# A two-layer AdaLN kernel on one core: the attention loop's work is put in another order

## The reference, cut to what matters

```
h = layernorm(x) * (1 + ca) + sa              # ca, sa per batch
q, k, v = h @ wq + bq, h @ wk + bk, h @ wv + bv    # 16 heads of 8
att = softmax(q k^T / sqrt(8)) v              # per head, 512 x 512 scores
x = x + ga * (att @ wo.T + bo)
h = layernorm(x) * (1 + cb) + sb
x = x + gb * experts0(h)                      # softmax router, top tokens per expert
...                                           # layer 1 follows: linear attention, 8 experts
```

## Time and profile before

| | us |
|---|---|
| median of 3 runs | 1118.73 |
| lowest and highest run | 1104.53, 1119.12 |
| span of the profiled execution | 1110.3 |
| busy: PE, PE weight loads | 929.3, 596.8 |
| busy: DVE, ACT, POOL | 759.5, 589.6, 460.1 |

### The profile page before, as it was taken

The page is one execution under the profiler, slowest core; times in us unless marked ns, Lnnn a source line. Parts: engine busy times, 40 slices in busy tenths (PEclk is TensorE's granted clock), DMA queues, the critical chain, the costliest instruction groups (busy, mean ns, idle before and its releaser), DMA issues. The chain is left out here.

```text
span 1110.3 us, 23738 instructions
## 1 busy us (share of the span) xinstructions
PE 929.3 (84%) x7248; PEld 596.8 (54%) x7248; DVE 759.5 (68%) x1948; ACT 589.6 (53%) x1257; POOL 460.1 (41%) x632
## 2 busy tenths in 40 slices
PE   5389898989798998997299899899898789987982
PEld 3023232323232333332298787788788779886761
DVE  2578797878688788889478856655656566663552
ACT  1048677777577676776034435525533475754551
POOL 5121222323231304130424446755752545765772
PEclk9999899999899899999589999999998899998996
DMA  4523232323150515170161001001100112223332
GB/s 134 134 102 88 103 97 98 102 92 108 39 153 14 166 35 168 36 240 12 47 237 58 16 16 34 28 24 30 31 18 18 47 38 61 70 62 106 107 93 76
DMA packets 56332, 87.09 MB, mean 78 GB/s; under 512 B 10388, under 2 KB 41186, under 8 KB 55568
## 3 DMA queue, kind: packets, MB, share of 16 engines
q1 hardware_dynamic: 45392, 53.75, 17.2%
q0 software_dynamic: 10816, 31.84, 8.0%
HBM read 45.83 MB, written 40.24 MB: 78 GB/s over the span
## 5 line engine op out<-in xcount | busy, mean ns | idle before, releaser
L680 DVE TENSOR_REDUCE nmax<-ps_s 128x1 f32<-128x512 f32 x512 | 321.8, 683 | 68.8 <-PE ps_s L861 67.1
L574 ACT ACTIVATE p_ring<-ps_t 128x512 f32<-128x512 f32 x512 | 286.8, 598 | 133.0 <-PE ps_t L872 130.1
L861 PE MATMUL ps_s<-k_stack,q_stack 56*128 56x512 bf16 x512 | 184.6, 409 | 35.2 <-DMA q_stack<-q_parts_dram 16.0
L872 PE MATMUL ps_t<-q_stack,k_stack 59*128 59x512 bf16 x512 | 188.0, 396 | 5.7 <-ACT p_ring L574 2.6
L885 PE MATMUL ps_av<-p_ring,v_ext 128*32 128x256 f32 x2048 | 168.1, 401 | 3.4 <-ACT att L584 2.3
L861 PEld LDWEIGHTS ps_s<-k_stack,q_stack 56*128 56x128 bf16 x512 | 39.9, 94 | 167.8 <-DVE nmax L680 92.0
L1408 POOL DMA_INDIRECT back_dram<-weights,target x78 | 88.3, 1132 | 73.6 <-DVE weights L2018 49.8
L1674 ACT ACTIVATE weights<-a,wtile 128x128 f32<-128x128 f32 x312 | 89.5, 374 | 36.5 <-PE a L2281 35.7
L2292 PE MATMUL a<-wtile,weights 128*128 128x128 f32 x624 | 86.1, 282 | 17.1 <-DVE weights L2018 9.8
L1581 ACT ACTIVATE hid<-a 128x512 f32<-128x512 f32 x64 | 38.2, 598 | 110.0 <-PE a L2103 109.7
L1422 POOL DMA_INDIRECT rows_dram<-hrow,slot x64 | 65.8, 1028 | 74.0 <-DVE y L1772 43.9
(11 more groups left out here) (277 smaller groups left out, 1500.6 us busy)
## 6 DMA issues: line engine op xcount, KB each, us to landing
rows_dram<-wmod POOLq DMA_DIRECT2D x8, 2340.0 KB, 8.5
k_stack<-k_parts_dram SPq DMA_DIRECT2D x32, 192.0 KB
q_stack<-q_parts_dram SPq DMA_DIRECT2D x32, 192.0 KB
xt<-rows_dram SPq DMA_DIRECT2D x78, 65.0 KB, 1.9
wall<-in_wall SPq DMA_DIRECT2D x1, 4112.0 KB, 13.4
q_parts_dram<-q_parts SPq DMA_DIRECT2D x32, 128.0 KB, 2.4
weights<-back_dram SPq DMA_DIRECT2D x8, 512.0 KB, 4.2
k_parts_dram<-k_parts SPq DMA_DIRECT2D x24, 128.0 KB, 2.3
```

Of the source, the lines that this page charges most:

```text
L574: nc.scalar.activation(probs[:, u % RING, :], ps_t[u % TBANKS][:], ACT.Exp, scale=HD ** -0.5).then_inc(exp_done, 1)
L680: nc.vector.tensor_reduce(nmax[:, js, n:n + 1], ps_s[u % SBANKS][:], AX.X, ALU.max, negate=True).then_inc(max_done, 1)
L861: nc.tensor.matmul(ps_s[u % SBANKS][:], q_stack[par][row:row + STACK, c, quarter(t)], k_stack[par][row:row + STACK, c, :], start=True, sto ...
L872: nc.tensor.matmul(ps_t[u % TBANKS][:], k_stack[par][rows_, c, quarter(t)], q_stack[par][rows_, c, :], start=True, stop=True).then_inc(t_f ...
```

## The change

The work of an iteration stands at other places, now named constants (`P_` for PE, `A_` for ACT, `D_` for DVE, with the value of u). `score_t`, the exponentials and `weigh` of unit v are issued on PE at u = v + `LEAD`, with LEAD = 2, so the last two of a batch fall into the next iteration; ACT still counts by its own v, and DVE by u. The statistics and the norm are those of the batch after the next (`statistics_1(nxt + 1)` at u = 31, `norm_1(nxt + 1)` on POOL between two `maxima`), those of batch 0 and 1 both in iteration -1. The projections stand at u = 4, 5 and 10. The copy of v into `v_ext` has moved from DVE to ACT (`save_values`), without the bias: PE computes bv @ wo.T once, DVE adds it to the output bias. Which heads `score` takes at a given u has changed with LEAD, so that `score` and `score_t` of one u still use opposite halves of PE's rows.

```diff
+LEAD = 2
+P_NT = 2
+P_K = 4
+P_Q = 5
+P_V = 10
+P_M1 = 6
+P_H3 = 8
+P_TT = 14
+P_O = 20
+P_M2 = 21
+P_H0 = 23
+P_N2 = 28
+P_LG = 31
+P_M3 = 40
+P_H1 = 44
+P_PT = 47
+P_M0 = 60
+P_H2 = 63
+A_H = 0
+A_K = 2
+A_Q = 5
+A_V = 11
+A_M1 = 4
+A_S3 = 3
+A_TT = 16
+A_S0 = 19
+A_M2 = 20
+A_N2 = 27
+A_S1 = 35
+A_LG = 37
+A_M3 = 40
+A_PT = 49
+A_S2 = 51
+A_M0 = 59
+D_K = 4
+D_Q = 7
+D_N3 = 9
+D_O = 20
+D_N0 = 26
+D_LG = 34
+D_S1 = 31
+D_RT = 45
+D_N1 = 51
+D_N2 = 63
+WEIGH = {1: 0, 3: 1}
+OPPOSITE = (0, 1, 2, 3)
...
-    return (v + 2) % HG
+    return OPPOSITE[v % HG]
...
-        bv = sb("bv", [P, P])
+        bv = sb("bv", [P, B])
...
-            iteration(Batch(B - 2), B % 2)
-            iteration(Batch(B - 1, after=False), (B - 1) % 2)
-            iteration(Batch(B, here=False, after=False), B % 2)
+            iteration(Batch(B - 2, ahead=False), B % 2)
+            iteration(Batch(B - 1, after=False, ahead=False), (B - 1) % 2)
+            iteration(Batch(B, here=False, after=False, ahead=False), B % 2)
...
-            sp.dma_start(bv[:], io["bv"].partition_broadcast(P)).then_inc(wqkv_in, 16)
+            sp.dma_start(bv[:], io["bv"]).then_inc(wqkv_in, 16)
...
 
             def iteration(it, par):
                 b, nxt, prev = it.own, it.own + 1, it.own - 1
-                if it.after:
-                    pool.wait_ge(mv1_done, nxt + 1)
-                    pool.wait_ge(hT_filled, nxt)
-                    norm(nc, half, x_all[:, nxt], mv1, rstd1, r1_step, nxt, xh1, xh1_ready)
+                def norm_1(m):
+                    pool.wait_ge(mv1_done, m + 1)
+                    pool.wait_ge(hT_filled, m)
+                    norm(nc, half, x_all[:, m], mv1, rstd1, r1_step, m, xh1, xh1_ready)
+
+                if it.after and not it.here:
+                    norm_1(0)
                 if it.after and not it.here:
 
                     pool.wait_ge(shift_mm, 1)
@@ -549,6 +598,8 @@
                     norm(nc, half, x_all[:, prev], mv2, rstd2, r2_step, prev, xh2, xh2_ready)
                 if it.here:
                     maxima(b, 3)
+                if it.ahead:
+                    norm_1(nxt + 1)
                 if it.after:
                     maxima(nxt, 0)
 
...
+                def save_values():
+                    act.wait_ge(v_filled, nxt + 1)
+                    if it.before:
+                        act.wait_ge(av_done, H * b)
+                    act.wait_ge(consts, 7)
+                    nc.scalar.copy(v_ext[1 - par][:, :, :, 0:HD],
+                                   bank_a[:].rearrange("p (t h e) -> p t h e", t=NT, h=H)).then_inc(v_ready, 1)
...
-                    work |= {3: lambda: save_av(prev, 3), 17: save_attT, 30: shift_h2, 37: exp_logits, 46: save_probT}
+                    work |= {A_S3: lambda: save_av(prev, 3), A_TT: save_attT, A_N2: shift_h2, A_LG: exp_logits, A_PT: save_probT}
-                    work |= {7: lambda: save_maxima(b, 1, bank_b), 22: lambda: save_maxima(b, 2, bank_b),
-                             38: lambda: save_maxima(b, 3, bank_b), 20: lambda: save_av(b, 0),
-                             35: lambda: save_av(b, 1), 51: lambda: save_av(b, 2)}
+                    work |= {A_M1: lambda: save_maxima(b, 1, bank_b), A_M2: lambda: save_maxima(b, 2, bank_b),
+                             A_M3: lambda: save_maxima(b, 3, bank_b), A_S0: lambda: save_av(b, 0),
+                             A_S1: lambda: save_av(b, 1), A_S2: lambda: save_av(b, 2)}
-                    work |= {8: shift_h, 10: lambda: first_part("k"), 13: lambda: first_part("q"),
-                             57: lambda: save_maxima(nxt, 0, bank_a)}
+                    work |= {A_H: shift_h, A_K: lambda: first_part("k"), A_Q: lambda: first_part("q"), A_V: save_values,
+                             A_M0: lambda: save_maxima(nxt, 0, bank_a)}
...
+                dve.wait_ge(shift_mm, 1)
+                nc.vector.tensor_tensor(vectors[:, 0, :], vectors[:, 0, :], bank_b[0:B, 2 * D:3 * D], ALU.add
+                                        ).then_inc(gate_step, 1)
+                dve.wait_ge(gate_step, 6)
-                dve.wait_ge(shift_mm, 1)
...
-                if it.after:
-                    if not it.here:
-                        dve.wait_ge(x0_in, 16)
-                    elif not it.before:
-                        dve.wait_ge(x_in, 16)
-                    dve.wait_ge(xh1_ready, nxt)
-                    statistics(x_all[:, nxt], st1, mv1, st1_done, mv1_done, nxt)
+                def statistics_1(m):
+                    if isinstance(m, int) and m < 2:
+                        dve.wait_ge(x_in if m else x0_in, 16)
+                    dve.wait_ge(xh1_ready, m)
+                    statistics(x_all[:, m], st1, mv1, st1_done, mv1_done, m)
+
+                if it.after and not it.here:
+                    statistics_1(0)
+                if it.ahead:
+                    work |= {D_S1: lambda: statistics_1(nxt + 1)}
-                    work |= {8: lambda: normalise(prev, 3, bank_b), 20: residual, 33: logits, 40: router}
+                    work |= {D_N3: lambda: normalise(prev, 3, bank_b), D_O: residual, D_LG: logits, D_RT: router}
-                    work |= {25: lambda: normalise(b, 0, bank_a), 43: lambda: normalise(b, 1, bank_a),
-                             59: lambda: normalise(b, 2, bank_b)}
+                    work |= {D_N0: lambda: normalise(b, 0, bank_a), D_N1: lambda: normalise(b, 1, bank_a),
+                             D_N2: lambda: normalise(b, 2, bank_b)}
-                    work |= {10: lambda: rest("k"), 14: lambda: rest("q"), 17: values}
+                    work |= {D_K: lambda: rest("k"), D_Q: lambda: rest("q")}
...
-                if t == 0 and i == 0:
+                if t == 0 and i != 1:
-                some = slice(T // 2 * i, T // 2 * (i + 1))
+                some = slice(0, T) if i is None else slice(T // 2 * i, T // 2 * (i + 1))
-                                            probs[:, (HG * k + g) % RING, some], start=(t == 0 and i == 0),
+                                            probs[:, (HG * k + g) % RING, some], start=(t == 0 and i != 1),
-                if i:
+                if i != 0:
...
-                    free((it.before, avT_read[3], prev + 1), (it.here, m_rows_ready[1], b + 1), (True, mod_ready, 3))
+                    free((it.before, avT_read[2], prev + 1), (it.here, grow_ready, 9), (True, mod_ready, 3))
+                    pe.wait_ge(rest_in, 48)
+                    last = nc.tensor.matmul(bank_b[0:B, 2 * D:3 * D], bv[:], wo[:], start=True, stop=True)
-                    free((it.after, k_rest_ready, nxt + 1))
...
-                    work |= {8: lambda: heads_T(prev, 3, bank_b, (it.here, m_rows_ready[1], b + 1),
+                    work |= {P_H3: lambda: heads_T(prev, 3, bank_b, (it.here, m_rows_ready[1], b + 1),
-                             17: tokens_T, 20: project_o, 30: norm2_T, 33: logits, 45: probs_T}
+                             P_TT: tokens_T, P_O: project_o, P_N2: norm2_T, P_LG: logits, P_PT: probs_T}
-                    work |= {6: lambda: maxima_T(b, 1, bank_b, (it.before, avT_read[2], b), (True, grow_ready, 9)),
-                             21: lambda: maxima_T(b, 2, bank_b, (it.before, attT_ready, prev + 1),
+                    work |= {P_M1: lambda: maxima_T(b, 1, bank_b, (it.after, k_rest_ready, nxt + 1), (True, avT_read[2], b)),
+                             P_M2: lambda: maxima_T(b, 2, bank_b, (it.before, attT_ready, prev + 1),
-                             26: lambda: heads_T(b, 0, bank_a, (it.before, x_ready, prev + 1),
+                             P_H0: lambda: heads_T(b, 0, bank_a, (it.before, x_ready, prev + 1),
-                             36: lambda: maxima_T(b, 3, bank_b, (it.before, h2T_ready, prev + 1),
+                             P_M3: lambda: maxima_T(b, 3, bank_b, (it.before, h2T_ready, prev + 1),
-                             41: lambda: heads_T(b, 1, bank_a, (it.before, lg_ready, prev + 1),
+                             P_H1: lambda: heads_T(b, 1, bank_a, (it.before, lg_ready, prev + 1),
-                             57: lambda: heads_T(b, 2, bank_b, (it.before, probT_ready, prev + 1),
+                             P_H2: lambda: heads_T(b, 2, bank_b, (it.before, probT_ready, prev + 1),
-                    work |= {4: norm_T, 9: project_k, 10: project_q, 15: project_v,
-                             53: lambda: maxima_T(nxt, 0, bank_a, (it.here, avT_read[1], b + 1),
+                    work |= {P_NT: norm_T, P_K: project_k, P_Q: project_q, P_V: project_v,
+                             P_M0: lambda: maxima_T(nxt, 0, bank_a, (it.here, avT_read[1], b + 1),
...
-                    if it.here:
-                        score_t(b, u, par)
-                    if u % HG in (1, 3):
-                        if u < HG and it.before:
-                            weigh(prev, H - 1, 1 - par, u % HG // 2)
-                        elif u >= HG and it.here:
```

(26 more changed lines are left out.)

## The result

The kernel after takes 1060.17 us (median of 4 runs, 1058.66 to 1061.46) against 1111.63 (median of 4, 1102.4 to 1119.12): a ratio of 0.9565, 95% interval 0.9521 to 0.9609. The profiled execution has a span of 1057.5 us against 1110.3, 52.8 less where 29.6 were forecast: 23.2 of the 29 us are gain that the sum missed, and 5.7 are its base, since the prediction put the median 8.4 us above the span and after it stands 2.7 above.

A forecast was written before the change was run, and what follows sets the result against it. Heads were taken as bound by PE with its waits and lower clock, rests by DVE. Gains 29.1 - 2.2 + 0.9 - 0.5 + 2.3 = 29.6 us took 1118.7 to 1089; range 1066 to 1108, likeliest case alone 1080 to 1098.

The forecast's parts named there:

- the sentence on the rest: Units 21 to 63 of an iteration: LEAD's shift of ACT's copies costs nothing, within plus and minus 0.27 us per iteration.
- It is DVE's: Units 21 to 63: DVE bounds them, 30.60 of 34.13 us busy; statistics add 1.27 us, the logits wait of 0.9 goes.
- Rival B: New places feed DVE in units 21 to 63 too: 1077 us if half of the other 24 goes, 1065 if all; chance 0.20.
- Both head waits: Units 0 to 20: PE's 1.68 us for the norm and 0.85 behind DVE's statistics both go.
- The 0.85 "behind DVE's statistics": Units 0 to 20: PE's wait of 0.85 us, put down to DVE's statistics, goes when they move to unit 31.
- The forecast of 19.2: New length of units 0 to 20: 17.9 us of PE work plus 1.3 kept, all at the upper clock; 21.76 before.
- Rival A: Clock still falls in every head, so five low heads gain only 2.6 us each: sum 18.7, time 1100 us; chance 0.17.
- Rival C: Stall moves to k's rest at unit 6 and q's at 10: 24 us given back, 1113 us; chance 0.11.
- Rival D: Next batch's row maxima land late: PE waits up to 1.7 us at each of 7 boundaries, up to 12 us; chance 0.06.
- The values on ACT: Head: v's copy moves from DVE to idle ACT, costed at nothing, 0.7 us a head without that cover.
- Iteration -1: Before the first scores: one more small PE product ahead of the signal POOL waits for, a loss of 0.5 us.
- The first picking round: Iteration 7: it no longer stands behind the logits, DVE's wait of 2.27 us goes, gain 2.3 us.

The follow-up runs named there:

- the first experiment: Kernel after with LEAD = 0, OPPOSITE = (2, 3, 0, 1) and ACT's small copies two units later: 1072.37 us, ratio 0.9665.

## Why the prediction was wrong, point by point

The step that failed is the sentence on the rest: "LEAD moves ACT's copies against DVE's extra work by two units; buffers and order within a unit stay. I cost it at nothing, with bounds of plus and minus 0.27 us per iteration". It looked at LEAD and priced with it, at nothing, some twenty moved places. These are worth 53.27 - 50.59 = 2.7 us an iteration, ten times the bound; the six rests and iteration 0 together came 13.1 + 3.2 = 16.3 us below their forecast, of the 23 that were missing. The bound came from half a unit, a size that has nothing to do with the question. The row that had it was quoted: 34.13 us of which DVE works 30.60 and PE 31.70. Two engines that work in order and wait for each other, at 90% and 93% of the stretch, can lose the difference to the order of their work; what a new order can give back goes up to their idle time, 2.4 us for PE and 3.5 for DVE, not to 0.27. The rest took in the 1.27 us of statistics and was still 1.9 us shorter. "It is DVE's" failed with it: in the new order the rest is as full on PE, and the statistics, for which the sum took 1.27 us each, cost 0.2 (32.18 in iteration 2, 31.98 in iteration 6 without them).

The other 5.7 us of the 29 are the base. The prediction added 8.4 us to the span because the median of three runs stood so far above it; with the fourth run the median before is 1111.63.

What the places change was narrowed, not settled. It isn't LEAD, nor the head, nor the length of ACT's copies, nor the unit at which DVE normalises the second heads. Each group of moved pieces has a share (1.0 early, 0.56 router, 0.77 maxima and third heads, the remainder of the 1.66 for the second heads or their meeting). Each group shows as one wait of PE, for another reader each time: 1.06 us for ACT's copy, 0.34 for ACT's exponential, 0.83 for DVE's maximum; the rest shows as scores that overlap less. I take the spacing of PE's own blocks for what lies behind the last two, at 41, 45, 53 and 57 in the old order, at 44, 47, 60 and 63 in the new. That is argued, not shown: no run took away one of these blocks, and none moved ACT's first copy or DVE's piece for the third heads alone.

Rival B had the mechanism and the price: DVE fed in the rest, 1077 if half of its idle time went, 1065 if all. It had 0.20. On the span its two prices are 1069 and 1057, and 1057.5 was measured. That it meets the second so closely is in part luck: 14.4 us of waits for scores are still there, and 2.4 us came from the second phase. I held against it that PE waits for both readers in order, as before, which is no argument about where its work stands.

The heads. Both head waits went, all ordinary heads run at 1.00, and 26.5 us of forecast stand against 28.7. But only the norm's wait went for the reason given. The 0.85 "behind DVE's statistics" is not the statistics' alone: with them moved PE still stood 0.76 us, and in the kernel after the old places of the maxima and the third heads bring 0.83 back. The forecast of 19.2 kept 1.3 us of small waits; the changed kernel has 18.2 to 18.7, since the projections' places, for which I allowed nothing, remove the 1.2 us before v. With the norm alone the head was 19.6.

Rival A, the clock. In ordinary heads the granted clock is 1.00. With q's wait put back (0.8 us on PE) it was 1.00 as well; with the norm's wait of 1.7 put back, 0.93. The Trainium skill (TensorE: Matmul & The Clock Gate, section "A second HAM failure mode: psum-queue depth-cycling") has a PE that pauses often and briefly swing between the levels. The trace disagrees here: in iteration 6's rest of the kernel before, PE stood 34.13 - 31.70 = 2.4 us in short pauses, the longest listed one 0.7 us, and the clock was 1.00. The kernel after tests it less, since its PE hardly pauses.

Rival C: the stalls moved to where it said, DVE before k's and q's rests, 9.4 and 4.1 us in seven iterations, but PE has other work there and stood 0.2 us. Rival D: the maxima land in time, 0.4 us of waits. The five units of its sum are right, from ACT's copy at u = 61 to the reader at 66, but LEAD does not eat two: without it the reader stands at 64, three units behind the copy, and the wait is there, as the first experiment shows.

The values on ACT: nothing, right. Iteration -1: I forecast 0.5 us of loss; the first score came at 44.11 against 45.72. Over the profiles of the experiments it lies between 43.40 and 46.25 without regard to the edits (later only, 47.58 and 48.23, in the two runs with short copies, which fill two tiles more at the start), so a term of that size can't be read. The first picking round: right, no wait stands ahead of it:

```profile
445.62 1.28 DVE L739 TENSOR_REDUCE nmax<-ps_s 128x1 f32<-128x512 f32 x2
446.81 0.68 DVE L167 MAX8 picks<-rows 48x8 f32<-48x512 f32 x1
```

The stretch gained 3.3 us where 2.3 were forecast. The second phase was 2.4 us shorter in this pair of executions; the change doesn't touch it, and I didn't look for the cause.

## What to carry to other kernels

Where two engines that work in order and feed each other are both nearly full in a stretch and neither is quite, a change of the order can be worth as much as their idle time there; price it between nothing and that, and never at nothing because the work is the same. From the old places to the new the rest lost 2.7 us, where PE had 2.5 idle and DVE 3.1; it can be more than the fuller engine's idle time, since PE's busy time fell too. Take such a change apart before believing any one cause: here the norm ahead gave 3.1 us an iteration, the head's places 1.2 and the rest's places 2.7, while the edit that names the change, the lead of two units, gave at most 0.34 and served to let a transfer start later.

## What the runs showed of the hardware

A jump back of a hardware loop cost 7.8 us in the kernel after, once: PE stood 2.74 and 2.25 us with no wait to show, and the head with it ran at a mean granted clock of 0.87. In the thirteen other traces that have the norm ahead and keep the loop, this iteration lasted 7.5 to 11.9 us longer than the one behind it. The Trainium skill (Runtime: NRT & Kernel Launch, section "Instruction fetch mechanics") says that a taken branch breaks the sequential prefetch of instructions, and that the engine stalls where the target is not at hand and has to be fetched. The runs agree as far as they go: the gap goes with the jump. That it is the fetch, no run here shows.
